# Routing operations between two scans, and guards before two GpSimd products of a step cycle

## The reference

```
S = S * exp(gt)[..., None] + kt[..., None] * vt[..., None, :]
ot = einsum('bhk,bhkd->bhd', qt, S)
```

## Time and profile before

| what | us |
|---|---|
| median of 3 runs | 553.41 |
| the profiled execution | 552.09 |
| its span | 549.9 |
| PE busy | 447.7 (81%) |
| DVE busy | 325.0 (59%) |
| ACT busy | 233.4 (42%) |
| POOL busy | 291.1 (53%) |
| GpSimd's products L571, 32 | 75.8 |
| VectorE's scans L1026, 64 | 75.0 |
| scatters L605, 64 | 62.7 |

### The profile page before, as it was taken

One profiled execution on the slowest core, in us unless ns is written; L12 is line 12 of the kernel. 1 busy time (PEld: TensorE's weight loads), 2 busy tenths in 40 slices (PEclk: granted clock), 3 DMA queues, 4 the chain that ended last, 5 costly groups with the idle time before them and its releaser, 6 DMA issues.

```text
span 549.9 us, 8864 instructions
## 1 busy us (share of the span) xinstructions
PE 447.7 (81%) x2189; PEld 260.9 (47%) x2190; DVE 325.0 (59%) x624; ACT 233.4 (42%) x527; POOL 291.1 (53%) x221
## 2 busy tenths in 40 slices
PE   2875984416496889889799989999999999999765
PEld 2331421004142543445464657767767767767422
DVE  5577676999799889983945623333333333333107
ACT  3533775000331133133544436556556655656403
POOL 4017677414688878877300016656666666666600
PEclk9977998555698999899999999999999999999969
DMA  8733677986353445335959546666666766664495
GB/s 249 223 123 108 220 275 242 357 309 195 129 186 129 147 133 192 116 106 165 382 177 261 115 155 98 112 105 111 104 104 115 110 107 108 109 109 55 52 284 192
DMA packets 73416, 90.29 MB, mean 164 GB/s; under 512 B 7752, under 2 KB 56488, under 8 KB 73384
## 3 DMA queue, kind: packets, MB, share of 16 engines
q1 hardware_dynamic: 53848, 66.05, 39.5%
q0 software_dynamic: 14448, 19.34, 20.6%
q10 hardware_dynamic: 5088, 4.50, 2.5%
HBM read 50.66 MB, written 39.21 MB: 163 GB/s over the span
## 4 chain that ended last, share of the span: by engine, by line
PE 60%; DVE 21%; issue 8%; DMA 4%; ACT 4%; POOL 2%; SPq 0%; DVEq 0%; ACTq 0%; POOLq 0%
PE mm_ps L327 33%; PE sum_ps L327 12%; DVE st L1026 4%; PE turn_ps L1346 3%; PE mm_ps L1453 3%; DVE kv L1018 3%; PE sum_ps L1324 2%; PE turn_ps L327 2%; DVE h_mlp L1155 1%; POOL qs L571 1%; PE mm_ps L1492 1%; DMA y_scratch<-y,X 1%; DMA vrep<-v_scratch 1%; PE turn_ps L1492 1%; PE turn_ps L1288 1%
## 5 line engine op out<-in xcount | busy, mean ns | idle before, releaser
L633 POOL DMA_INDIRECT y_scratch<-y,X x79 | 123.1, 1558 | 133.9 <-ACT y L868 86.2
L327 PE MATMUL mm_ps<-w_gu,xT 128*128 x474 | 102.5, 352 | 1.6 <-DVEq L1236 1.5
L571 POOL TENSOR_TENSOR qs<-st,q_sb 128x1024 f32<-128x1024 f32 x32 | 75.8, 2370 | 40.6 <-DVE st L1026 38.5
L1146 DVE TENSOR_TENSOR xT<-turn_ps,xT 128x256 f16<-128x256 f32 x79 | 33.4, 424 | 87.7 <-ACT xT L779 87.7
L327 PE MATMUL sum_ps<-wd,hT 112*128 x316 | 81.4, 380 | 0.1
L1026 DVE TENSOR_TENSOR_SCAN st<-sum_ps,kv 128x512 f32<-128x512 f32 x64 | 75.0, 1208 | 2.7 <-POOL qs L571 1.8
L605 POOL DMA_INDIRECT rows_scratch<-rows,slot_u x64 | 62.7, 980 | 17.3 <-issue 16.6
L327 PE MATMUL mm_ps<-an2T,w 128*128 128x512 f16 x264 | 64.5, 400 | 9.1 <-DVE h_mlp L1155 6.7
L327 PEld LDWEIGHTS mm_ps<-w_gu,xT 128*128 128x128 f16 x474 | 46.0, 97 | 32.6 <-issue 2.7
L1324 PE MATMUL sum_ps<-qs,sumk 128*32 128x512 f32 x128 | 39.0, 692 | 27.4 <-POOL qs L571 27.2
L1241 DVE SCALAR_TENSOR_TENSOR h<-mm_ps,X,sl 128x224 f32<-128x224 f32 x79 | 35.6, 450 | 40.5 <-ACT sl L852 40.5
(11 more groups left out here) (176 smaller groups left out, 533.6 us busy)
## 6 DMA issues: line engine op xcount, KB each, us to landing
vrep<-v_scratch SPq DMA_DIRECT2D x64, 256.0 KB
rows_scratch<-zrow SPq DMA_DIRECT2D x20, 548.0 KB, 7.5
X<-rows_scratch SPq DMA_DIRECT2D x80, 137.0 KB, 2.6
w_gu<-y_scratch SPq DMA_DIRECT2D x16, 256.0 KB, 6.5
y_scratch<-zrow ACTq DMA_DIRECT2D x6, 640.0 KB, 10.6
w_gu<-in_L_ffn_gate_proj_dram SPq DMA_DIRECT2D x16, 224.0 KB, 5.8
w_gu<-in_L_ffn_up_proj_dram SPq DMA_DIRECT2D x16, 224.0 KB, 6.0
wd<-in_L_ffn_down_proj_dram SPq DMA_DIRECT2D x1, 3136.0 KB, 17.5
```

The lines of the kernel that those rows point to most:

```text
L327: last = nc.tensor.matmul(out_ap, lhsT, rhs, start=(n == 0), stop=(n == len(pairs) - 1))
L571: nc.gpsimd.tensor_tensor(qs[:, u % 2, :, :], st[:, u % 2, :, :], pair_bc(q_sb[:, TOK(a)]), ALU.mult).then_inc(s["qs_ready"], 1)
L633: nc.gpsimd.indirect_dma_start(y_dram[u % 2], bass.IndirectOffsetOnAxis(ap=X[:, u, TOKEN_C:TOKEN_C + 1].bitcast(U32), axis=0), y[:, u, :], ...
L1146: nc.vector.tensor_tensor(xT[:, u % 2, 1, :, :].rearrange("p c n -> p (c n)"), PS[u % 2][:, 0:KC * P], xT[:, u % 2, 0, :, :].rearrange("p ...
```

## The change

The recurrence pieces are grouped otherwise: at the start product and first scan of step 0, then six chained routing operations, then the second scan together with product and first scan of step 1, four operations, and so on; `BETWEEN_SCANS` counts the operations between a step's two scans. Of the last 20, eleven are there, and the second scan of step 3 then comes after the slot numbers.

GpSimd's scatters get counts by step. From batch b = 1 on, its product of step 3 waits for the head chain of the same iteration, and in every iteration its product of step 6 waits for the row chain. The other lines name a constant.

```diff
         SCATTER_FROM = 5
+        HEAD_STEPS = 4 + 3 * NEWTON
+        SCATTERS = (2, 3, 4, 2, 3, 4, 3, 3)
+        FIRST_SCATTERS = (2, 1, 3)
...
                     if u == 0:
                         pool.wait_ge(s["evac_act"], len(ACT_NTH) * a + ACT_NTH[Q_OUT])
+                    if b and u == 3:
+                        pool.wait_ge(s["head_dve"], (b + 1) * HEAD_STEPS)
+                    if u == 6:
+                        pool.wait_ge(s["row_rstd"], b + 1)
                     product(a, u)
...
-                if b is not None and (b > 0 or u >= SCATTER_FROM):
-                    scatter(2 if b == 0 else 3)
+                if b == 0 and u >= SCATTER_FROM:
+                    scatter(FIRST_SCATTERS[u - SCATTER_FROM])
+                if b:
+                    scatter(SCATTERS[u])
...
-            BESIDE = 4
+
+            BETWEEN_SCANS = (6, 4, 3, 20)
+            BESIDE = len(BETWEEN_SCANS)
...
             def recurrences_beside_routing():
-                for u in range(BESIDE):
-                    yield from recurrence(1, u)
-                    yield
+                for u, operations in enumerate(BETWEEN_SCANS):
+                    rec = recurrence(1, u)
+                    for _ in range(2):
+                        next(rec)
+                    for _ in range(operations):
+                        yield
+                    for _ in rec:
+                        pass
 
             beside = recurrences_beside_routing()
             step = sem_chain(dve, s["dve_chain"], step(None), between=lambda: next(beside, None))
+            next(beside)
...
-                        chain = sem_chain(dve, s["head_dve"], 0, 4 + 3 * NEWTON, b)
+                        chain = sem_chain(dve, s["head_dve"], 0, HEAD_STEPS, b)
```

## The result

The changed kernel takes 548.1 us (median of 4 runs, 547.14 to 549.34) against 553.58 for the kernel before beside it; the ratio is 0.9915, with a 95% interval from 0.9887 to 0.9943. By this ratio it is 4.7 us less (3.2 to 6.3). The forecast was 1.2 us less, and the time lies under the forecast range. Run again with the kernel before on the same chip it gave 0.9918 (0.989 to 0.9945); one execution of the kernel before, at 1820 us, far from all others, is left out there. The profiled execution shows a span of 546.2 us against 549.9, 3.7 less. The traced execution of the kernel before took 552.09 us, 1.5 under its median, and that of the changed kernel 548.29, 0.2 over its own: the two traces together can't show the whole difference, and where in the kernel the other microsecond arises is in no trace.

What follows compares the result with a forecast made beforehand. VectorE mostly bounds 86 to 254 us, TensorE afterwards. The shift is +1.4 us at the second iteration's start and -1.2 after the third: span 549.9 to 548.7, time 552.2 against 553.41, range 549.6 to 555.0.

Steps and rivals of the forecast that it cites:

- the sum: Shifts carried through the iterations: +1.4 us at the second's start, -1.2 by its second MLP addition, -1.2 after the third.
- Start of the second iteration +1.4: Second iteration begins 1.4 us later, because TensorE's readout 6 and transposes wait for product 6 at the low clock.
- Part 1: Routing stage: operations placed between two scans avoid GpSimd's products; product 3 then hits the head chain; yields 0.2 to 0.3 us.
- The price of product 6: First iteration: product 6 starts behind the row chain, so readout 6 and transposes come late; subtractions end at 149.9 against 148.56.
- a sign of being wrong: Iterations shorter than 49 us, listed among the observations that would show the forecast wrong.
- the faster rival: No clock loss at product 6, GpSimd's loop of 48.8 us is the floor; 549.5 to 550.9 us; chance 0.37.
- Part 2: Product 6 behind the row chain: +1.4 us in iteration 1; later TensorE gains about 0.1, and 1.5 at the next gate product.
- Part 3: Scatter counts and product 3's wait: products 2, 4 and 5 come 1.27 us earlier relative to product 0; the wait costs nothing.
- land where they did: Second iteration: products 4 and 5 keep their old times, and so do TensorE's w2 products.
- The slower one: Product 6's wait becomes TensorE idle time at readout 6 ahead of the transposes; 555.9 to 557.2 us; chance 0.16.
- The third: Guards never bind and products 5 and 2 still hinder the chains; -0.3, 553.1 us; chance 0.47 together with the forecast.
- Its rule on descriptors: GpSimd can't write scatter descriptors while VectorE is in a two-port mode; scatters before the chains would stretch; no term given.

Runs made afterwards that it cites:

- the last version: Changed kernel with readout of step 6 behind transposes and w2 products, last second scan before the maxima, slot numbers behind the first head chain's reduction; ratio 0.9829, 543.79 us.
- filler: 18 matmuls with unread results added on TensorE in iteration 1, ahead of the readout of step 4, to the kernel before; ratio 0.9993.
- readouts last: Changed kernel with TensorE's readout of step 6 moved behind the transposes and the last w2 products of step 7; ratio to the kernel before 0.9869.
- the filler with the POOL edits: Kernel before plus the two GpSimd waits, the scatter counts and 18 unread matmuls ahead of the readout of step 4 in iteration 1; ratio 0.9924.
- the POOL edits alone: Kernel before plus only the two GpSimd waits and the scatter counts, routing as before; ratio 0.9905.

## Why the prediction was wrong

**The failing step is the sum's first line, "Start of the second iteration +1.4".** It was -0.7 at the low parts and -1.0 at the head scalar of iteration 2. The error of about 2 us in the trace lies before 147 us, in two terms.

- *Part 1, 0.3 forecast, 0.9 measured.* The slot numbers came 0.5 us earlier than worked out (115.3; the bias addition lost 0.4 to GpSimd's subtraction, not 0.7), product 3 began at 116.6 instead of 117.05, and the stretched scalar was done at 119.0 instead of 119.6. The collision itself was as forecast, 1.26 us of stretch, and it could be had back (the last version).
- *TensorE's clock, nothing forecast, 1.3 us measured.* I carried the `Wo` products through at 5.75 us. In every kernel with the routing edit they took 4.3 to 4.9, in the two without it and without filler 5.75 and 5.78. TensorE reads out product 3 at 119.02 there, and waits 2.3 us ahead of the transposes; before, it had waited 9.7 us since the readout at 112.46. The row chain's start moved by 2.1, 0.9 of it from part 1. The filler shows that what TensorE did ahead sets these products' time. That exactly the moved readout does it is my reading; no run moved it alone, and it is not the whole: with the same order on TensorE they took 4.29 (readouts last) and 4.91 (the last version), and with readout 3 still later, close to the transposes, 4.92. That the shorter products are worth something behind them the filler with the POOL edits shows: 2.1 us off the group, 1.5 at the low parts.

*The price of product 6 was right in size.* The forecast has 2.3 us from the end of the row chain to the subtractions (-0.9 to +1.4); it was 2.2 (-2.9 to -0.7), with the readout at 1.92 and the transposes at 1.97 us. The forecast missed that the clock is high behind it: the granted clock was 0.50 in readout and transposes (142.3 to 146.1 us) and 1.00 in the first gate products, which took 2.76 us instead of 4.03.

*Behind the low parts the sum held, but in part by luck.* The forecast had 2.6 us to win there (+1.4 to -1.2), and the traces show 2.6 in iteration 2 (-0.7 to -3.3) and 0.2 in iteration 3. The forecast carried 1.1 us from the head chain on to the row chain; the trace has -1.9 behind the head scalar but -1.0 at the row chain's start, because the gate products of step 4 took 5.28 us for 4.34. From the row chain's start to the additions the forecast had 1.5 us and the trace 2.3. From the low parts of iteration 1 to those of iteration 2 is 48.0 us, and on to those of iteration 3 49.0, against 50.6 and 49.8 before. The first is under 49, which the forecast named as a sign of being wrong, and under the 48.8 that the faster rival took for a floor.

*Part 2 in iteration 2*: chain 2.36 us instead of 5.22, transposes 4.7 us behind its end where 5.1 were forecast (I had taken 1.63 for the transposes, which was ScalarE's pace; behind a late readout all rows are ready and they take 1.09).

*Part 3* was underrated. The head scalar lost 0.5 us to product 2 in iteration 2 and 1.5 in iteration 3, where 0.35 and 0.8 were forecast. The sum gave the counts only the 1.1 us at the first of these scalars, since products 4 and 5 "land where they did". Without the counts the change keeps 0.2% of its 0.85%, with the reservation above on the clock's share.

*The rivals.* The faster one was right in its premise, no loss at the start of iteration 2, for another reason than the one named (the clock was low at product 6), and its time of 549.5 to 550.9 is still over the measured one. The slower one has its mechanism in the table (2.2 us at the readout), but the chain paid for it. The third, waits that never bind, is true of product 3 alone. The rest of the miss, from 3.4 us of R to 4.7 timed, stays open as to its place in the kernel. It is no more than the traced execution of the kernel before lies under its median (1.5 us), and with the POOL edits alone the same gap is larger.

The Trainium skill's rule ("SBUF — State Buffer", Who interferes with whom) fits every stretched VectorE operation shown here, product 3 with the head scalar (1.45 us) among them. Its rule on descriptors, which I gave no term, cost nothing where the scatters lie beside the chains (0.96 to 1.01 us each).

## What to carry to other kernels

When one engine's work is moved off another's chain, ask who reads its result in program order. The wait for product 6 was worth nothing while its readout stood ahead of the transposes, and 1% of the time once that readout was last; try such edits in pairs. Put no more weight on one trace than its least steady group allows: one group of twelve matmuls took 2.76 to 5.30 us here. Where TensorE stands idle for some microseconds ahead of a critical group, don't carry the group through at its old length.

## What was not expected of the hardware

- The same sixteen `Wo` products took 3.72 to 5.78 us and the same twelve gate products 2.76 to 5.30. For the first the filler shows that it is what TensorE did before. Ahead of the gate products stands the same wait of 2.5 us in nearly all traces, so the wait alone does not tell their length, and no run shows what does.
- A product that follows a scatter without a wait blocks VectorE before its own recorded start: without the wait for product 6 one operation began at 186.86 and took 2.89 us, while the product is recorded from 187.37 to 189.72. The scatters before it, at 185.12 and 186.39, left the same chain's operations at 0.16 to 0.17 us.
- A scatter that begins after a VectorE subtraction of 128x896 with two inputs in SBUF (1.09 us) has begun takes longer by most of what is left of it. Begun 0.06 us behind it, it took 1.86 us instead of 0.96, in six of the fourteen traces; with the readouts last 1.76 and 1.23 (begun 0.16 and 0.68 behind), in the last version 1.60 and 1.22 (0.32 and 0.68). One that began ahead of the subtraction kept 0.96 to 0.99, by as little as 0.06 us in the second trace of the changed kernel. Order of time on VectorE, then on GpSimd, of the changed kernel:

```profile
261.18 1.09 DVE L1155 TENSOR_TENSOR w_gu<-w_gu 128x896 f16<-128x896 f32 x1
```

```profile
261.24 1.86 POOL L608 DMA_INDIRECT rows_scratch<-rows,slot_u  x1 [0.30 <-issue]
```
